# The mask of the first self-attention moved to ScalarE, with the residual of the group ahead between its two halves

## The reference, cut to what matters

```python
def self_attn(x, Wq, Wk, Wv):
    Q, K, V = (x @ Wq, x @ Wk, x @ Wv)
    energy = jnp.einsum('bqd,bkd->bqk', Q, K)
    lengths = jnp.sum(energy[:, 0] != 0, axis=-1)
    pad = kidx[None, None, :] >= lengths[:, None, None]
    causal = (kidx[None, :] > kidx[:, None])[None]
    energy = jnp.where(pad | causal, NEG_INF, energy)
    score = jax.nn.softmax(energy / np.sqrt(DK), axis=-1)
    return jnp.einsum('bqk,bkd->bqd', score, V)
...
z = self_attn(x, Wq1, Wk1, Wv1)
x = layer_norm(x + z, ln1_g, ln1_b)
z = cross_attn(x, context, Wq2, Wk2, Wv2)      # 1444 keys
```

## Time and profile before

| what | value |
|---|---|
| median of 3 runs | 2162.99 us |
| lowest and highest | 2161.19 and 2169.7 us |
| the profiled execution | 2172.06 us, of it 2170.3 us span |
| mean granted TensorE clock | 0.924 |
| busy share of the span, PE / DVE / ACT / POOL | 89% / 68% / 61% / 31% |
| stretch of the 8 groups, first norm to first matmul of the cross attention | about 28 to 135 us of the span |

### The profile page before, as it was taken

One profiled execution on the slowest core, in us unless ns is written; L12 is line 12 of the kernel. 1 busy time (PEld: TensorE's weight loads), 2 busy tenths in 40 slices (PEclk: granted clock), 3 DMA queues, 4 the chain that ended last, 5 costly groups with the idle time before them and its releaser, 6 DMA issues. The chain is left out here.

```text
span 2170.3 us, 42902 instructions
## 1 busy us (share of the span) xinstructions
PE 1935.4 (89%) x16792; PEld 1224.2 (56%) x16792; DVE 1481.8 (68%) x3509; ACT 1321.2 (61%) x2169; POOL 670.7 (31%) x605
## 2 busy tenths in 40 slices
PE   3669999766899999999999999999998899999997
PEld 2536766444465656656566565665655455555553
DVE  4844666785778787777877778777783456577541
ACT  2635677586166666666666666666776345666643
POOL 1410223321422131322313223131221323566576
PEclk9879999877599999999999999999999557999998
DMA  5025555001232332323323232232332102221222
GB/s 157 1 69 189 168 186 172 26 27 47 89 106 82 114 119 72 131 82 114 108 84 131 81 115 97 95 131 68 124 105 75 24 12 45 48 41 36 36 70 42
DMA packets 126293, 190.74 MB, mean 88 GB/s; under 512 B 42018, under 2 KB 99466, under 8 KB 125710
## 3 DMA queue, kind: packets, MB, share of 16 engines
q1 hardware_dynamic: 126094, 188.01, 27.9%
HBM read 104.84 MB, written 11.76 MB: 54 GB/s over the span
## 5 line engine op out<-in xcount | busy, mean ns | idle before, releaser
L1607 DVE TENSOR_REDUCE b_part_max<-psum 128x1 f32<-128x482 f32 (+3 forms) x1248 | 738.6, 650 | 200.8 <-PE psum L1493 186.0
L1413 ACT ACTIVATE b_PT<-psum 128x800 f32<-128x800 f32 x768 | 614.9, 836 | 335.4 <-PE psum L1512 329.5
L1493 PE MATMUL psum<-b_KH,b_QBD 64*128 64x482 f32 (+1 forms) x1152 | 416.2, 441 | 37.4 <-DVE b_part_max L1607 35.0
L1512 PE MATMUL psum<-b_QS,b_KS 64*128 64x200 f32 x3072 | 436.7, 288 | 0.3 <-ACT b_PT L1413 0.3
L1512 PEld LDWEIGHTS psum<-b_QS,b_KS 64*128 64x128 f32 x3072 | 346.2, 187 | 15.2 <-issue 10.5
L1528 PE MATMUL psum<-b_PT,b_V 128*32 128x200 f32 x6144 | 341.4, 339 | 0.3 <-ACT b_PT L1413 0.3
L1493 PEld LDWEIGHTS psum<-b_KH,b_QBD 64*128 64x128 f32 x1152 | 194.1, 189 | 182.1 <-DVE b_part_max L1607 115.7
L1338 POOL TENSOR_TENSOR b_KL<-b_KF,b_KH 128x1444 fp32r<-128x1444 f32 x32 | 106.9, 3340 | 589.7 <-PE psum L1512 566.5
L1528 PEld LDWEIGHTS psum<-b_PT,b_V 128*32 128x32 f32 x6144 | 159.9, 109 | 144.6 <-ACT b_PT L1413 78.7
L1814 POOL TENSOR_TENSOR c_HE<-c_HE,c_G 128x400 f32<-128x400 f32 x128 | 131.5, 1032 | 112.6 <-ACT c_HE L1960 106.0
L426 POOL TENSOR_TENSOR a_rs<-a_ve,a_half 100x4 f32<-100x4 f32 x48 | 48.5, 1011 | 312.6 <-DVE a_ve L918 312.5
(11 more groups left out here) (280 smaller groups left out, 2988.2 us busy)
## 6 DMA issues: line engine op xcount, KB each, us to landing
b_KS<-b_KH SPq DMA_DIRECT2D x64, 722.0 KB
a_CT<-in_ctxt SPq DMA_DIRECT2D x32, 722.0 KB, 5.6
b_CT<-in_ctxt SPq DMA_DIRECT2D x32, 722.0 KB, 4.3
b_KS<-b_KL SPq DMA_DIRECT2D x32, 722.0 KB
a_CN<-in_ctxn SPq DMA_DIRECT2D x32, 704.0 KB
c_G<-gates_scratch SPq DMA_DIRECT2D x16, 800.0 KB, 4.3
att_scratch<-b_AO SPq DMA_DIRECT2D x32, 200.0 KB, 5.8
b_MB<-in_mask SPq DMA_DIRECT2D x32, 180.5 KB, 4.4
```

The costliest lines, as they stand in the source:

```text
L1413: nc.scalar.activation(PT[:, kt % 2, 2 * a:2 * a + 2, :], psum[:, 2 * a:2 * a + 2, 0:TG], ACT.Exp).then_inc(sem["pt_ready"], 1)
L1493: m = mm(bank(b, D, size), QBD[rows, j % 2, tile * D:(tile + 1) * D], KH[rows, j % 2, at_:at_ + size], start=True, stop=True)
L1512: m = mm(bank(p, D, 2 * T, (s % 2) * 2 * T), KS[rows, j % 2, s, kt * D:(kt + 1) * D], QS[rows, j % 2, s * 2 * T:(s + 1) * 2 * T], start=Tr ...
L1607: v.tensor_reduce(part_max[0:rows, q, c:c + 1], bank(b, rows, CHUNKS[c][1]), AX.X, ALU.max)\
```

## The change

`mask_scores` no longer builds the mask. A new step `keep_lengths` on VectorE writes minus `CUT` times the four lengths to `sm[:, p, 3, :]`; a new step `cut1` on ScalarE makes the mask from it with four activations, one for each sequence, as `Relu(-CUT * base - CUT * length)` into `E1`; and `mask_scores` subtracts that from the scores. On VectorE, `residual1` of the group ahead is moved up: it stands between `lengths` and `keep_lengths`.

```diff
+            def cut1(u):
+                p = u % 2
+                act.wait_ge(sem["lens_ready"], u + 1)
+                for j in range(GROUP):
+                    last = nc.scalar.activation(E1[:, p, j, :], K[0:T, K_BASE:K_BASE + T], ACT.Relu, scale=-CUT,
+                                                bias=sm[:, p, 3, j:j + 1])
+                last.then_inc(sem["cut1_ready"], 1)
...
-                   (turned0, 0), (turned1, 3), (exponent1, 1), (rotated2, 3), (rotated1, 0), (weights1, 1)), UNITS + 3)
+                   (turned0, 0), (turned1, 3), (cut1, 1), (exponent1, 1), (rotated2, 3), (rotated1, 0), (weights1, 1)), UNITS + 3)
...
+            def keep_lengths(u):
+                p = u % 2
+                dve.wait_ge(sem["len1_psum"], u + 1)
+                ts(sm[:, p, 3, :], bank(3 + p, T, GROUP, TG), -CUT, None, ALU.mult).then_inc(sem["lens_ready"], 1)
+
             def mask_scores(u):
...
-                dve.wait_ge(sem["len1_psum"], u + 1)
-                link(v.tensor_copy(s[:, 3, :], bank(3 + p, T, GROUP, TG)))
-                base = K[0:T, K_BASE:K_BASE + T].unsqueeze(1).to_broadcast([T, GROUP, T])
-                link(v.tensor_tensor(E, base, s[:, 3, :].unsqueeze(2).to_broadcast([T, GROUP, T]), ALU.add))
-                link(ts(E, E, 0.0, CUT, ALU.min, ALU.mult))
-                link(v.tensor_tensor(E, s1, E, ALU.add))
+                dve.wait_ge(sem["cut1_ready"], u + 1)
+                link(v.tensor_tensor(E, s1, E, ALU.subtract))
                 link(v.tensor_reduce(s[:, 0, :], E, AX.X, ALU.max))
...
-            ticks(((enter, 0), (lengths, 1), (mask_scores, 1), (residual1, 2)), UNITS + 2)
+            ticks(((enter, 0), (lengths, 1), (residual1, 2), (keep_lengths, 1), (mask_scores, 1)), UNITS + 2)
```

More of the change, by code:

```diff
@@ L105 @@
 A_SIGNALS = """
-a_chain a_cleared a_out_ready aqT_psum aqT_ready aq_ready down_psum e1T_psum e1T_ready e1_ready e2_ready eg_ready
-f1_psum f1_ready f2_psum factors_ready gu_psum gu_used hout_ready inner_ready len1_psum len1_ready len2_ready
+a_chain a_cleared a_out_ready aqT_psum aqT_ready aq_ready cut1_ready down_psum e1T_psum e1T_ready e1_ready e2_ready eg_ready
+f1_psum f1_ready f2_psum factors_ready gu_psum gu_used hout_ready inner_ready len1_psum len1_ready lens_ready len2_ready
 max2_ready pT_psum pT_ready quant_ready r2_psum rT2_ready rT_ready r_psum row_ready s1_psum s2_psum s2m_psum scaled1
```

## The result

The changed kernel takes 2172.99 us in the median of 20 runs against 2164.13 us for the kernel before (20 runs). The ratio is 1.0035, with a 95% interval of 1.0018 to 1.0052: slower by 3.9 to 11.3 us, 7.6 in the middle (the medians themselves lie 8.9 us apart). The single runs scatter by far more than that, from 2164.94 to 2190.25 us in the changed kernel and from 2160.54 to 2184.02 before, so the stretch of the 8 groups is read from the profiles, where its ticks repeat closely.

A forecast was written before the change was run, and what follows sets the result against it. Bound in stage A's pipeline: a loop through GpSimd's gain, TensorE's turn, ScalarE's copies and norm. Six turns +4.0 us and two first ticks +2.1 make +6.1 on 2162.99, so 2169.1 us; range 2162 to 2175.5.

The forecast's parts named there:

- the loop: Stage A's 8-group pipeline, one `normalise(1)` to the next: 11.52 us against 10.85, +4.0 us over six turns.
- the cuts' price: Four Relu passes added on ScalarE in each tick: 1.18 us, bounds 0.49 and 1.94 us.
- the first two ticks: Ticks without gain at the pipeline's start: first `normalise(1)` +2.1 us later, 0.92 of it from tick 1.
- from the gain's end to the copy of `turned1`: Term of the new tick's sum, between GpSimd's gain and ScalarE's second turned copy: 1.03 us.
- The residual's new place is hidden: VectorE in full ticks: `residual1` moved up lies hidden behind GpSimd's gain, with 1.3 us to spare.
- GpSimd gets its 0.22 us back: GpSimd's second gain instruction in full ticks: 1.26 us instead of 1.48 without the mask beside it.
- All that follows only shifts: After the pipeline: the drain keeps its 16.19 us, and everything from the cross attention's first matmul on only shifts.
- a changed length behind 141 us: Sign of a wrong prediction: something after the cross attention's first matmul, expected near 141.3 us, changes its length.
- the cuts cost next to nothing: Rival on ScalarE's added passes: cuts at 0.49 us, sum +0.6 us, 2163.6 us; chance of under +3: 0.15.
- VectorE's time sets the tick: Rival: VectorE's chain closes each tick, so removing the mask saves 18.5 us, 2144.5 us; chance 0.04.
- passes through no instruction of `mask_scores`: Old tick's loop of gain, turn to copy, copies and norm, 10.7 us: claimed to contain no mask instruction.
- VectorE is just shorter: Old full tick: VectorE's chain would have let `normalise(1)` start at about 108.2 us instead of 108.50.

The follow-up runs named there:

- order_only: Kernel before, with the residual moved between the counting and the mask on VectorE; ratio to before 1.0017, first cross-attention matmul at 133.41 us.
- early_old: Changed kernel with cuts ahead of both turned copies, lengths' write early, residual behind the mask; ratio to before 0.9990, first matmul 133.99 us.
- early_mid: Changed kernel with cuts ahead of both turned copies, lengths' write ahead of the residual, subtraction after it; ratio to before 0.9986, first matmul 131.84 us.
- cut_twice: Changed kernel with four more Relu passes ahead of the cuts, written to an unread tile; 2179.63 us in one execution, first matmul 150.79 us.

## Why the prediction was right, point by point

**The sign and the size.** 2169.1 us was predicted, 6.1 above before; the ratio gives 7.6, and the difference lies within the interval. The measured median, 2172.99 us, is 3.9 above the one named. The mechanism of the loop and the cuts' price were right. That the terms met the measured 6.12 us of the first matmul so closely was luck: the loop was put too high by 1.4 us, and the first two ticks too low by as much in that profile.

**The loop.** Its mechanism held in each step: the cuts behind the second copy, the subtraction behind the cuts, the exponentials behind that. It was put at 11.52 us and measured 11.28 (11.09 to 11.46 in single ticks, half of them below the 11.3 to 11.7 that were named). The term that was too large is "from the gain's end to the copy of `turned1`", 1.03 us from a tick of the drain, where TensorE had the low clock (0.50 from 118 to 125 us). In the tick above it is 0.65 us (95.77 to 96.42), in the six ticks 0.65 to 1.02 and 0.86 on average; the rest are hundredths in the other terms. So six turns cost 2.6 us over before, not 4.0.

**The cuts' price.** 1.18 us was taken from the exponentials' rows, 1.18 was measured in every tick. Of the Trainium skill, "ScalarE: Activation LUTs", section "What ACT_TABLE_LOAD costs", gives 280 ns and 0.833 ns for each element with a bias from SBUF, which makes an estimate of 363 ns for 100, and 93 ns of overlap. The trace agrees, with 369 ns in the mean of 32, and with 0.10 us of overlap (four of 0.369 less 1.18, over three).

**The first two ticks.** They were put at 2.1 us; by the starts of the first `normalise(1)` they measured 3.5, and 2.9 in the second profiles. Counted from the first count it is 18.94 us against 15.68, 3.3 more, and in the second profiles 17.73 against 15.75, 2.0 more. So the term is right in one pair and too small in the other. The VectorE of the changed kernel in the first pair:

```profile
47.09 0.56 DVE L935 TENSOR_SCALAR a_P<-psum 1x400 f32<-1x400 f32 x1 [2.10 <-PE psum L698]
...
48.79 0.18 DVE L956 RECIPROCAL a_sm<-a_sm 100x4 f32<-100x4 f32 x1 [0.55 <-PE psum L707]
```

The count of tick 2 starts 1.62 us later than before instead of the 0.92 that I carried over (0.26 of that is the later start of the stretch), and the residual, now next in line, waits 0.55 us for TensorE's `weigh1` (L707), which I had not looked at. From this count to the first `normalise(1)`, in the changed kernel's first profile and then in its second:

```profile
47.09:57.40 10.31, 7.69 (x32) 6.05 (x32) 6.67 (x33) 5.42 (x20) 2.41 (x4) 0.50 0.00 1
```

```profile
46.79:56.46 9.67, 5.04 (x32) 4.03 (x33) 6.58 (x33) 5.99 (x21) 2.42 (x4) 0.92 0.00 1
```

The same 32 matmuls have a granted clock of 0.50 in one and 0.92 in the other (before, 45.47 to 53.88, it is 1.00). Just ahead of the count the eight matmuls of L698 take 1.50 us in the first and 0.94 in the second, and in the second the reciprocal doesn't wait for L707. So what the term missed is TensorE's clock in these ticks, which can come out either way in one kernel.

**The residual's new place is hidden.** Right: the lengths were written at 95.93 and the second copy left ScalarE at 96.81, 0.9 us later (1.3 was estimated). In the first full tick the room is only 0.04 us (62.81 and 62.85), in the others 0.9 to 1.25. order_only shows that the place alone costs 0.8 us in the first ticks and gives back more in the full ones. L925 was held by the gain as foreseen, 0.34 us.

**GpSimd gets its 0.22 us back.** Right, 1.27 us, but order_only has the same without removing anything: the collision was a matter of where the mask stood, not of its being there.

**All that follows only shifts.** Not quite, and the prediction had named a changed length behind 141 us as a sign of being wrong. From the first matmul to the first exponential of stage B (L1413, now L1422) it is 463.3 us before in both profiles and 465.2 and 465.1 in the changed kernel. 0.8 us of the 1.9 lie ahead of the last matmul of the scores (260.9 us against 261.7) and 1.1 between it and stage B (202.4 against 203.5). These 1.9 us on top of the 6.1 (5.6) of the pipeline make 8.1 and 7.4 us, the size of the measured ratio. That the change causes them is not shown: the same length is 469.4 and 463.3 us in the two profiles of early_old, which has the cuts as well, and up to 473.3 in early_mid.

**The rivals.** That the cuts cost next to nothing fell with cut_twice. That VectorE's time sets the tick fell for the changed kernel and for early_mid, with 6.58 us of VectorE in a tick of 9.27 or 11.43. For the kernel before it fell only in part. The loop that the prediction added up, which "passes through no instruction of `mask_scores`", is that of the tick from 97.75 to 108.50, with the granted clock at 0.84. In the tick from 76.02 to 86.48, with the clock at 1.00, the four copies were done about 1 us before the norm, and the norm waited for GpSimd's last small instruction, which stands behind VectorE's mask and residual:

```profile
86.48 1.65 ACT L475 ACTIVATE a_Y<-a_U,a_nb,a_rs 100x128 f32<-100x128 f32 x4 [1.02 <-POOL a_nb L428]
```

The norm at 118.95 waited 1.17 us for the same instruction. So before the change two of the six distances were closed through VectorE. The sum of the prediction doesn't suffer, since it starts from the measured 10.85 us, but the reading "VectorE is just shorter" holds for the tick that was read and not for all. In the changed kernel none of the six norms waits for GpSimd.

## What to carry to other kernels

An engine that is busiest in a stretch need not bound it: add up the loop that closes from one step of the pipeline to the same step of the next tick, across engines, before moving work off the busy one, and do it for more than one tick, since another loop can close the next one. Work moved to another engine costs by its place in that engine's program: the same four instructions cost 4.0 to 5.0 us more behind a copy that is waited for than ahead of it. And where two instructions slow each other, moving one can end that without removing it: L938 and L939 take 0.97 us instead of 2.69. When single profiles are compared, count from the same event of the stretch, not from the start of the span.

## What the runs showed of the hardware that was not expected

early_mid's gain of 3.3 us in the pipeline can't be seen further on: stage B starts at 605.1 us of the span there and at 598.4 before. Two later stretches have lengths of their own. The first is the quantised feed-forward, from the last matmul of the scores to stage B; before, and in early_mid:

```profile
396.00:598.40 202.40, 142.86 (x624) 89.38 (x622) 151.86 (x450) 106.29 (x206) 61.74 (x60) 0.70 0.14 47
```

```profile
394.60:605.10 210.50, 158.27 (x624) 98.78 (x622) 152.37 (x450) 107.32 (x206) 61.79 (x60) 0.63 0.13 45
```

With the same 624 matmuls the stretch is 8.1 us longer, at a granted clock of 0.63 instead of 0.70. early_mid's second profile has 207.9 us there at 0.65, early_old 208.5 at 0.65 and in its second profile 202.4 at 0.71. The second stretch is the start of stage C, 150 us from the last exponential of stage B; before, and in the changed kernel:

```profile
1670.70:1820.70 150.00, 129.21 (x821) 78.19 (x810) 77.54 (x200) 60.56 (x102) 40.08 (x38) 0.56 0.15 33
```

```profile
1678.80:1828.80 150.00, 124.10 (x904) 74.94 (x896) 84.01 (x213) 67.24 (x112) 48.05 (x46) 0.67 0.19 44
```

At 0.67 it gets 83 matmuls further in the same time. From the last exponential of stage B to the end it is 499.6 us before and 489.4 in this execution of the changed kernel, and 502.8 in its second profile with the clock at 0.54 in its first 150 us (span 2180.7); before, the second profile has 502.8 as well. That is why the profiled changed kernel was shorter than the one before, and the difference is larger than all that the change moves. Stage B between them took 1072.2 to 1072.6 us in every profile. What decides which clock these two stretches get was not tried, and whether the clock alone makes their lengths is not shown.
